# A decoder layer on one core: the last pairs' chain reordered, the last pair's sums in their own buffer, and the experts' weight rests moved from VectorE to GpSimd

## The reference, cut to what matters

```python
x = layernorm(x + attention(x, Wq, Wkv, Wo, bo))              # 16 heads of 64, softmax over 128 keys
x = layernorm(x + mlstm(x, ctx, ctx, gates, rms_scale))       # 4 heads of 64
x = layernorm(x + moe(x, gamma, beta, Wr, br, W1, b1, W2, b2))

# mlstm, one head: log_d = cumulated log forget gates + input gate, masked by tri
m = max(log_d, axis=-1);  d = exp(log_d - m)
c = q @ k.T / sqrt(64) * d
h = c / (max(sum(c), exp(-m)) + 1e-6) @ v
h = h * rsqrt(mean(h ** 2) + 1e-6) * (1 + rms_scale)

# moe: 8 experts, F = 1024, the two best of a softmax over xn @ Wr + br
xn = layernorm(x) * gamma + beta
out = x + sum over the two of score * (relu(xn @ W1[e] + b1[e]) @ W2[e] + b2[e] ...)
```

## Time and profile before

| | |
|---|---|
| median of 3 runs | 795.53 us (795.30 to 795.84) |
| the profiled execution | 798.12 us, of it span 796.3 us |
| granted TensorE clock, mean over the span | 0.938 |
| busy over the span: TensorE, VectorE, ScalarE, GpSimd | 91%, 59%, 42%, 30% |
| the drain | 382 to 455 us of the span |

### The profile page before, as it was taken

How to read it: one execution, slowest core, us unless ns; L and a number is a source line. 1 busy time by engine, 2 the same in 40 slices (tenths; PEclk the granted TensorE clock), 3 DMA queues, 4 the chain that set the end, 5 groups by cost and what they waited for, 6 DMA issues and landing times.

```text
span 796.3 us, 15373 instructions
## 1 busy us (share of the span) xinstructions
PE 723.6 (91%) x5160; PEld 620.2 (78%) x5161; DVE 471.6 (59%) x1079; ACT 332.2 (42%) x989; POOL 240.2 (30%) x193
## 2 busy tenths in 40 slices
PE   4799999999999999997889999999999999997671
PEld 4688787888888897987789978888888888886330
DVE  3243446577868777778788455555555555554354
ACT  4566667676767666675432022122222222222011
POOL 2200000121405041232454570770374003300772
PEclk9899999999999999997968999999999999999555
DMA  8348385201110010102423252352154112100342
GB/s 305 88 165 295 130 294 178 58 15 41 41 42 28 28 54 2 61 7 85 142 80 100 92 176 71 119 171 92 60 171 145 40 40 66 39 28 21 99 146 73
DMA packets 62510, 77.41 MB, mean 97 GB/s; under 512 B 5836, under 2 KB 54520, under 8 KB 62456
## 3 DMA queue, kind: packets, MB, share of 16 engines
q1 hardware_dynamic: 53832, 47.29, 18.4%
q0 software_dynamic: 8608, 29.37, 11.6%
q10 hardware_dynamic: 16, 0.01, 0.0%
HBM read 45.04 MB, written 31.62 MB: 96 GB/s over the span
## 4 chain that ended last, share of the span: by engine, by line
PE 75%; ACT 6%; DVE 6%; issue 5%; POOL 4%; DMA 1%; another core or an unknown queue 1%; POOLq 0%; SPq 0%; DVEq 0%; ACTq 0%
PE bank L955 14%; PE bank L707 8%; PE bank L709 7%; PE bank L708 7%; PE bank L925 5%; PE bank L927 4%; PE bank L926 4%; PE bank L827 4%; PE bank L935 4%; PE bank L898 4%; PE bank L864 3%; PE bank L876 3%; ACT arena L1062 3%; POOL arena L697 2%; DMA work<-in_L_attn_Wkv_dram 1%
## 5 line engine op out<-in xcount | busy, mean ns | idle before, releaser
L955 PE MATMUL bank<-w_ring,hidT_hi 128*128 x320 | 119.8, 408 | 3.3 <-DVE hidT_lo L1587 3.3
L1180 ACT ACTIVATE hidT_hi<-bank 128x512 fp32r<-128x512 f32 x80 | 43.6, 596 | 174.6 <-PE bank L935 174.6
L1062 ACT ACTIVATE arena<-bank,negmx 128x128 f32<-128x128 f32 x256 | 91.0, 378 | 6.6 <-DVE negmx L1217 6.5
L955 PE MATMUL bank<-w_ring,hidT_lo 128*128 x320 | 83.3, 281 | 0.0
L1560 DVE TENSOR_TENSOR arena<-bank,b_rep 128x512 f32<-128x512 f32 x80 | 55.3, 692 | 39.2 <-PE bank L927 38.9
L1566 DVE TENSOR_REDUCE work<-bank 128x256 f32<-128x512 f32 x40 | 27.7, 692 | 79.4 <-PE bank L955 79.4
L955 PEld LDWEIGHTS bank<-w_ring,hidT_hi 128*128 128x128 f32 x320 | 60.1, 188 | 15.0 <-issue 4.0
L925 PE MATMUL bank<-w_ring,xgT_hi 128*128 x160 | 66.7, 417 | 4.6 <-DVE xgT_lo L1579 2.8
L1223 DVE RECIPROCAL rinv<-rsum 128x8 f32<-128x8 f32 x32 | 6.5, 203 | 95.9 <-ACT arena L1062 91.2
L927 PE MATMUL bank<-w_ring,xgT_lo 128*128 x160 | 62.9, 393 | 0.0
L926 PE MATMUL bank<-w_ring,xgT_hi 128*128 x160 | 62.5, 390 | 0.0
(11 more groups left out here) (243 smaller groups left out, 1902.4 us busy)
## 6 DMA issues: line engine op xcount, KB each, us to landing
xg_dram<-zeros SPq DMA_DIRECT2D x9, 2176.0 KB, 8.6
w_raw<-in_L_ffn_W_dram POOLq DMA_DIRECT2D x16, 1024.0 KB, 6.4
work<-xg_dram SPq DMA_DIRECT2D x40, 128.0 KB, 2.0
y_dram<-work SPq DMA_DIRECT2D x40, 128.0 KB, 1.7
b_rep<-in_L_ffn_b_dram POOLq DMA_DIRECT2D x8, 512.0 KB
work<-gmax_dram SPq DMA_DIRECT2D x14, 256.0 KB, 3.6
arena<-in_x_dram SPq DMA_DIRECT2D x8, 256.0 KB, 2.7
xres<-in_x_dram SPq DMA_DIRECT2D x1, 2048.0 KB, 15.4
```

The source lines that it names most:

```text
L955: last = pe.matmul(o, l, r, start=c == 0 and l is both[0], stop=c == FC - 1 and l is both[0])
L1062: last = nc.scalar.activation(probs[:, n % 2, h * S:(h + 1) * S], ps_score[:, h * S:(h + 1) * S], ACT.Exp, bias=negmx[:, n % 2, h:h + 1], ...
```

## The change

Four things change, and nothing of what is computed.

1. The order of DRAIN on TensorE, with other numbers of fillers ahead of the units (119 between the units and 55 at the end before; 80 and 40 after), and ScalarE's and VectorE's orders to match.
2. The sums of Z are kept in a buffer of their own, over the area pT that attention has left, so that ScalarE's copies of U for Z wait for nothing. That area lies where half (1,1) of the expert weights goes, so round_early of expert 1 now waits for var2_ready of Z.
3. GpSimd makes all four early rests, each followed by the load of the next expert's half.
4. GpSimd's order: both masks of Y first, scale_xn(A) after rstd_of_pair(Z), the rest (0,0) ahead of the masks of Z, scatter(A) after them, the rest (0,1) right behind both_norms(Z).

```diff
+        u2 = [area.rearrange("p (n e) -> p n e", e=AUG) for area in (carve(arena2, 2 * KC * AUG), pT[:, 0:2 * KC * AUG])]
...
-        DRAIN = [("w", Z, 1, 0), ("C", Z), ("w", Z, 1, 1), ("N", A), ("T", Y), ("L", A), ("X", Z), ("U", Y, 0), ("G", Z),
-                 ("R", A), ("U", Y, 1), ("T", Z), ("B", Z), ("S", Z), ("U", Z, 0), ("U", Z, 1), ("N", Y), ("L", Y),
-                 ("R", Y), ("N", Z), ("L", Z), ("R", Z)]
+        DRAIN = [("w", Z, 1, 0), ("C", Z), ("w", Z, 1, 1), ("T", Y), ("X", Z), ("U", Y, 0), ("G", Z), ("U", Y, 1), ("N", A),
+                 ("L", A), ("B", Z), ("S", Z), ("T", Z), ("R", A), ("U", Z, 0), ("U", Z, 1), ("N", Y), ("L", Y), ("N", Z),
+                 ("L", Z), ("R", Y), ("R", Z)]
...
+            def rest_early(e, part):
...
+                pool.wait_ge(w_rounded, 2 * e + part + 1)
+                pool.tensor_tensor(both[:, :, 1, :], w_raw[:, part * KC * F:(part + 1) * KC * F]
+                                   .rearrange("p (g n) -> p g n", n=n), both[:, :, 0, :].bitcast(F32), ALU.subtract)\
+                    .then_inc(w_split, 1)
+                pool.wait_ge(w_split, 2 * e + part + 1)
+                load_raw(e + 1, part)
...
-            scale_xn(A)
-            rstd_of_pair(Z)
             for b in range(2):
                 mask(Y, b)
+            rstd_of_pair(Z)
+            scale_xn(A)
             load_bias(1)
-            scatter(A)
             head_norm(Y)
-            load_after_first(0)
+            rest_early(0, 0)
             for b in range(2):
                 mask(Z, b)
+            scatter(A)
             both_norms(Y)
+            head_norm(Z)
             scale_xn(Y)
-            load_after_first(1)
-            head_norm(Z)
             both_norms(Z)
+            rest_early(0, 1)
             load_bias(2)
             scatter(Y)
             scatter(Z)
-            rest_of_second()
+            for part in range(2):
+                rest_early(1, part)
...
-            pauses = {("N", A): 10, ("T", Y): 4, ("L", A): 6, ("R", A): 3, ("U", Z, 0): 22, ("R", Y): 20, ("N", Z): 34,
-                      ("R", Z): 20}
+            pauses = {("X", Z): 14, ("L", A): 3, ("B", Z): 5, ("R", A): 4, ("U", Z, 0): 3, ("N", Y): 24, ("L", Y): 3,
+                      ("N", Z): 5, ("L", Z): 3, ("R", Y): 8, ("R", Z): 8}
...
-            fill(55)
+            fill(40)
...
-                    if p > 0:
+                    if 0 < p < Z:
                         act.wait_ge(var2_ready, p)
...
+            copy_unit(("X", Z))
+            for b in range(2):
+                copy_unit(("U", Y, b))
+            soft_gates(Z)
             copy_unit(("N", A))
-            copy_unit(("X", Z))
+            exp_of_m(Z)
             choice_exp(A)
-            copy_unit(("U", Y, 0))
-            soft_gates(Z)
-            copy_unit(("U", Y, 1))
-            exp_of_m(Z)
             copy_unit(("S", Z))
...
             copy_unit(("N", Y))
+            copy_unit(("N", Z))
             choice_exp(Y)
+            act.wait_ge(var2_ready, PAIRS)
             for part in range(2):
                 round_early(1, part)
-            copy_unit(("N", Z))
             choice_exp(Z)
...
-            both_norms(A)
             read_wo(Z, 1)
             moments(Z)
+            weigh(Y)
             normalise(Z)
-            weigh(Y)
-            rest_early(0, 0)
+            both_norms(A)
+            head_sums(Y)
+            read_gates(Z)
+            gate_sums(Z)
             logits_in(A)
             choose(A)
-            read_gates(Z)
+            weigh(Z)
             find_slots(A)
-            gate_sums(Z)
-            head_sums(Y)
             add_heads(Y)
-            weigh(Z)
+            head_sums(Z)
             both_norms(Y)
-            rest_early(0, 1)
-            head_sums(Z)
+            add_heads(Z)
+            both_norms(Z)
             logits_in(Y)
             choose(Y)
-            add_heads(Z)
             find_slots(Y)
-            both_norms(Z)
-            rest_early(1, 0)
             logits_in(Z)
             choose(Z)
             find_slots(Z)
```

More of the change, by code:

```diff
@@ L147, in decoder_layer @@
         AUG = P + 2
-        u = carve(arena2, 2 * KC * AUG).rearrange("p (n e) -> p n e", e=AUG)
+        u2 = [area.rearrange("p (n e) -> p n e", e=AUG) for area in (carve(arena2, 2 * KC * AUG), pT[:, 0:2 * KC * AUG])]
         gmax, softp = [carve(arena2, 2 * S)[0:XH, :] for _ in range(2)]
@@ L383, in decoder_layer, with u_of @@
         A, Y, Z = PAIRS - 3, PAIRS - 2, PAIRS - 1
-        DRAIN = [("w", Z, 1, 0), ("C", Z), ("w", Z, 1, 1), ("N", A), ("T", Y), ("L", A), ("X", Z), ("U", Y, 0), ("G", Z),
-                 ("R", A), ("U", Y, 1), ("T", Z), ("B", Z), ("S", Z), ("U", Z, 0), ("U", Z, 1), ("N", Y), ("L", Y),
-                 ("R", Y), ("N", Z), ("L", Z), ("R", Z)]
+        DRAIN = [("w", Z, 1, 0), ("C", Z), ("w", Z, 1, 1), ("T", Y), ("X", Z), ("U", Y, 0), ("G", Z), ("U", Y, 1), ("N", A),
+                 ("L", A), ("B", Z), ("S", Z), ("T", Z), ("R", A), ("U", Z, 0), ("U", Z, 1), ("N", Y), ("L", Y), ("N", Z),
+                 ("L", Z), ("R", Y), ("R", Z)]
+        def u_of(p):
+            return u2[p == Z]
         def step(s):
@@ L562, in load_bias @@
                 pool.dma_start(b1_rep[:, e % RING, :], b1[e:e + 1, :].broadcast_to([P, F])).then_inc(b1_loaded, 16)
[L564 to L577, removed]
+            def rest_early(e, part):
+                n = (512, D)[part]
+                both = w_ring[:, e, part * W_WORDS:(part + 1) * W_WORDS].rearrange("p (g k n) -> p g k n", k=2, n=n)
+                pool.wait_ge(w_rounded, 2 * e + part + 1)
[4 more added lines that the diff above has]
+                load_raw(e + 1, part)
             def split(e, part):
@@ L1044, in copy_unit @@
                     b, = a
-                    if p > 0:
+                    if 0 < p < Z:
                         act.wait_ge(var2_ready, p)
                     u_b = src[:, 0:KC * AUG].rearrange("p (c e) -> p c e", c=KC)
-                    nc.scalar.copy(u[:, KC * b:KC * (b + 1), :], u_b)
+                    nc.scalar.copy(u_of(p)[:, KC * b:KC * (b + 1), :], u_b)
                     nc.scalar.activation(xn_all[:, 2 * p + b, :].rearrange("p (c e) -> p c e", c=KC), u_b[:, :, 1:P + 1],
@@ L1302, in weigh @@
                         .then_inc(ring_free[place[un][odd][0]], 1)
-            u_v = u[:, :, 1:P + 1].rearrange("p n (z e) -> p n z e", z=2)
             def head_sums(p):
@@ L1311, in head_sums @@
                     heads = slice(z, None, 2)
-                    last = dve.tensor_tensor(den[:, heads], u[:, :, z * (P + 1)], gtok[:, p % 2, 2 * XH + z::2], ALU.max)
+                    last = dve.tensor_tensor(den[:, heads], u_of(p)[:, :, z * (P + 1)], gtok[:, p % 2, 2 * XH + z::2], ALU.max)
                 chain.link(last)
@@ L1322, in add_heads @@
                 h2 = xres[:, 2 * p:2 * p + 2, :]
+                u_v = u_of(p)[:, :, 1:P + 1].rearrange("p n (z e) -> p n z e", z=2)
                 dve.wait_ge(rsq_ready, p + 1)
@@ L1329, in add_heads @@
                 h4 = h2.rearrange("p b (c e) -> p (b c) e", c=KC)
-                chain.link(dve.tensor_tensor(h4, h4, u[:, :, 1:P + 1], ALU.add))
+                chain.link(dve.tensor_tensor(h4, h4, u_of(p)[:, :, 1:P + 1], ALU.add))
                 for b in range(2):
@@ L1425, in find_slots @@
                 dve.tensor_copy(slot[:, :, pair], row_f[:, :, pair]).then_inc(slot_ready, 1)
-            def rest_early(e, part):
-                n = (512, D)[part]
-                both = w_ring[:, e, part * W_WORDS:(part + 1) * W_WORDS].rearrange("p (g k n) -> p g k n", k=2, n=n)
-                dve.wait_ge(w_rounded, 2 * e + part + 1)
-                dve.tensor_tensor(both[:, :, 1, :], w_raw[:, part * KC * F:(part + 1) * KC * F]
-                                  .rearrange("p (g n) -> p g n", n=n), both[:, :, 0, :].bitcast(F32), ALU.subtract)\
-                    .then_inc(w_split, 1)
             attn_w = ((wq_hi, wq_lo[:, :, :], wq_raw), (wkv_hi[:, :, 0:INNER], wkv_lo[:, :, 0:INNER], wk_raw),
```

## The result

The changed kernel takes 800.79 us (median of 5 runs, 799.54 to 804.32) beside 795.53 for the kernel before (median of 5 runs measured beside it): ratio 1.0081 [1.0049, 1.0113]. It is slower, by 5 to 7 us. The profiled execution took 800.39 us, its span 798.6 us, and the mean granted clock over the span fell from 0.938 to 0.930.

A forecast was written before the change was run, and what follows sets the result against it. TensorE's start of the first tile was taken as the bound, behind overrunning fillers and VectorE's chain. Held by two rests, it moves from 454.63 to 462: +7.4 on the 795.5 median, so 803; own range 799 to 806.5.

The forecast's parts named there:

- The holds: GpSimd's rests (0,0) and (0,1), about 4.5 us each, make VectorE wait in gate_sums and both_norms(Z); chance 0.70.
- the bounds on the loss: VectorE's loss beside a GpSimd rest: 0.88 to 1.0 of the overlap, or nothing as other bound; upper end taken.
- Until gate_sums: VectorE's chain to the running maximum: gate_sums stands behind rest (0,0) until 402.9, maximum at 404.8 instead of 401.4; cost 3.4.
- the rivals without holds: Both rivals in which rests on GpSimd do not delay VectorE: no change (chance 0.14) or faster (chance 0.16).
- The start: On VectorE, moments go ahead of both_norms(A), so normalise(Z) ends at about 389.3 instead of 390.36.
- Neither the new order nor the buffer for u is worth anything by here: At var2_ready(Z), 429.6 against 429.18 before: rest (0,0) and idle time ahead of weigh(Z) eat the savings; cost 0.4.
- Until the slots: Rest (0,1) holds both_norms(Z) up to 4.3 us, TensorE falls to clock 0.50; slots of Z at 452.1, before 443.54: cost 8.5.
- Until the first tile: From slots, scatter and load give 461.1; 40 fillers take 9.0 to 18 us, ending at 463 with some loss; first tile 462.
- behind that: After the first tile: GpSimd's two later rests, loads and split end some 9 us later, covered by 27.45 us idle.
- the case that the clock stays up: TensorE keeps full clock: R(Y) at 442.5, slots at 449, first tile at 458.1, time 799.
- Rivals one and two: Rests hold nobody: one has first tile at 454.5, 796, no change, chance 0.14; two is faster, 791.4, chance 0.16.
- rival two: No holds, and half (1,1) or the exponential not late: fillers' overrun given back, first tile 450.5, -4.1, 791.4; chance 0.16.

The follow-up runs named there:

- e6: The changed kernel with only the rest (0,1) back on VectorE, behind gate_sums(Z): 796.98 us, ratio 1.0033 to the kernel before.
- e2: The kernel before, old order kept, with only its rests (and their loads) moved to GpSimd: 798.75 us, ratio 1.0037.
- e7: The changed kernel with only the rest (0,0) back on VectorE, behind both_norms(A): 799.38 us, ratio 1.0065 to the kernel before.
- e5: The changed kernel with rests (0,0) and (0,1) on VectorE, other filler counts, and ScalarE's copy of N(A) ahead of soft_gates(Z): 791.50 us, ratio 0.9958.
- e12: The changed kernel measured and profiled once more, nothing edited: 800.88 us beside 794.22 for the kernel before, ratio 1.0086.
- e1: The changed kernel with both rests (0,0) and (0,1) back on VectorE, GpSimd only issuing the loads: 799.02 us, ratio 1.0035 to the kernel before.
- e9: The kernel before with fewer fillers: 24 for 34 ahead of N(Z), 16 for 20 ahead of R(Z), 44 for 55 at the end: 790.83 us, ratio 0.9962.
- e10: e5 with the sums u of Z again in the same buffer as those of Y: 795.25 us, ratio 1.0020 to the kernel before.
- e11: The changed kernel, rests left on GpSimd, with e5's fillers and copy order, but 38 fillers ahead of N(Y) and 32 ahead of N(Z): 798.94 us, ratio 1.0063.

## Why the prediction was right, and where its sum was not

The forecast was 803 and slower; 800.8 was measured, inside the forecast's own range. Taken step by step:

**The holds are as foreseen.** VectorE stood through both rests (4.10 and 4.46 us for instructions of 0.34 and 0.16): it lost 3.76 of the 3.96 us and 4.30 of the 4.44 us in which they overlapped, so the upper end of the bounds on the loss was the right one. e6 and e2 show it by experiment. The Trainium skill's rule of an exclusive lock for the whole instruction (page "SBUF — State Buffer", section "Who interferes with whom") agrees with these rows, also where it says that writes alone hold only some kinds of VectorE instruction: beside the 1.80 us of zeros the two-input instruction of 128x2 took 0.16, the 128x256 tensor_scalars 1.99. It doesn't agree for GpSimd's short powers, and there the measurement decides (last section).

**"Until gate_sums", cost 3.4: over-sized.** The running maximum came as long after normalise(Z) as foreseen (15.5 us), and the hold took 3.76 us from VectorE. But on the path it cost 0.6 (B in e7, within the spread of two profiles) to 1.7 us (the time that TensorE stood ahead of B), since TensorE's L(A) and five fillers at half clock would have kept B waiting until 400.6 anyway. The prediction looked at VectorE's queue alone here. That doesn't move its own sum, but it makes the rivals without holds too fast. Only e5, which also mended TensorE, got B at 19.5 instead of 22.5.

**The start: normalise(Z) was placed too late.** Put at 389.3, it ended at 386.63 (385.90 + 0.73). Of the 2.7 us, 1.3 are only the earlier start of the whole profile after. The rest is the order: both_norms(A) now stands behind normalise(Z), and weigh(Y) fills the wait of 0.82 us for its norm. From there the working held: 40.3 us to var2_ready(Z) predicted (389.3 to 429.6), 40.1 measured (to 426.75). In it, scale_xn(Y) held VectorE for 2.4 us, as put down (2.11 us at 419.38 where 0.73 is usual, 1.17 at 421.53 where 0.17 is). All later stages are early by the same 2.6 to 3.3 us, and the first tile by 3.7. "Neither the new order nor the buffer for u is worth anything by here" was nearly right: counted from the start of read_wo(Z, 1), var2_ready(Z) came at 46.9 us, before at 47.3.

**"Until the slots": the mechanism held.** Rest (0,1) cost VectorE 4.3; TensorE went to 0.50; R(Y) stood behind its eight slow fillers for 2.2 us after its counts (2.5 predicted). From var2_ready(Z) to the slots of Z 22.2 us (426.75 to 448.96) against 22.5 predicted. ScalarE's last rounding ended at 441.11, ahead of the last exponential at 443.64, so the half (1,1) waited for nothing there, with 2.5 us to spare.

**"Until the first tile": right.** From the slots to the first tile 9.4 us against 9.9. The 40 fillers took 10.81 us, between the bounds 9.0 and 18, and ended at 458.49, as TensorE took the first tile at 458.33; by the load alone (issued at 455.68) it would have been 0.3 us sooner, if that takes the 2.3 us of e12.

**The last term, "behind that": nothing, as foreseen.** The first tile moved by 5.0 to 5.8 us from the start of the drain, the median by 5.3 and 6.7 in the two comparisons. From the first tile to the end of the span the profile after takes 340.3 us, before 341.7, e12 341.6. The two rests behind the scatter kept TensorE from nothing: its second tile starts 0.50 us after VectorE's part of it, as it does elsewhere. What e12 lost in its first tiles (1.65 us) the first profile doesn't have. Single profiles lie up to 2.7 us from their median.

**What was luck.** Counted from the last instruction of add_heads ahead of the drain, the first tile came 5.0 us later than before, where the sum had 7.4: 1.3 us were given back at the start, the rest are the small differences above. That the slots (448.96) and the first tile (458.33) fall on the figures given for the case that the clock stays up (449 and 458.1) is chance, for the clock did fall, and the earlier start of the profile made up for it.

**Rivals.** Rivals one and two had the rests hold nobody; rows and e6 exclude it. But e1 shows that without holds the kernel still isn't faster (1.0035), which rival two's 791.4 had not seen: it took TensorE as free when VectorE was ready. e5's ratio of 0.9958 is near that rival's (791.4 / 795.5, 0.995), reached only once fillers and ScalarE's order fitted too, and e9 reached as much in the old order. The buffer of its own is worth 0.6% in e5 (e10), most of it by way of TensorE's clock, and was never tried alone in the old order. Nor was GpSimd's new order: the power of both_norms(Y) starts at 417.44, right behind scatter(A), which before was done at 405.3, and what that costs isn't shown.

## What to carry to other kernels

A long GpSimd instruction that reads SBUF is to be counted as time of VectorE too, even if a small instruction meets it; it belongs where VectorE has nothing on the path, or works out of PSUM. Fillers are right only for one timing: after each edit of such a chain, look at each unit's idle time and at the length of the fillers ahead of it, for too few let the clock fall and too many, or the same number at half clock, make the unit late. Two slips can hide one another: the rests mended alone gave 0.46%, the fillers alone nothing that can be told, both 1.2%. And try the cheapest edit on the old kernel first: three filler counts (e9) gave as much as the whole change after its mending (e5).

## What the runs showed of the hardware beyond what was expected

- A 128x2 instruction was held for 4.46 us, and instructions of 128x8 in e2 for 4.50 and 4.37, by one GpSimd instruction of 4.5; a one-input tensor_scalar of 4x256 was held too (4.10).
- Not every GpSimd instruction holds. In the changed kernel a two-input VectorE instruction ran at its usual length within a power on GpSimd, and one with an input in PSUM within a rest:

```profile
418.49 1.63 POOL L606 TENSOR_TENSOR rsq<-ssq,neghalf 128x8 f32<-128x8 f32 x1
418.53 0.17 DVE L1346 TENSOR_TENSOR rboth<-rstd 128x2 f32<-128x2 f32 x1 [0.69 <-POOL rstd L610]
...
459.69 4.57 POOL L573 TENSOR_TENSOR w_ring<-w_raw,w_ring 128x2048 fp32r<-128x2048 f32 x1
463.82 0.41 DVE L1568 TENSOR_TENSOR xgT_lo<-bank,xgT_hi 128x256 fp32r<-128x256 f32 x1
```

- Cut in four, the same GpSimd work took 5.28 instead of 4.50 us, and VectorE was held anew by each piece (1.22, 2.77 for two instructions, 1.70 where 0.16, 0.74 and 0.69 are usual).
- A gap ahead of N(Y) of 1.46 us (e5) left the clock at 1.00, one of 2.94 (e10) was followed by 0.66 and then 0.50 in the windows from 420 and 422 us, and the 16 fillers ahead of N(Z) took 6.70 instead of 3.82 us. One of 2.22 us ahead of N(Z) (e11) left N(Z) at full length (0.63 us).
